# A two-layer graph attention kernel: folding W1 with the attention vectors on TensorE before the edge counts, and two reorderings on VectorE

## Chip, cores and metric

The kernel runs on one NeuronCore of a Trainium2 chip. The metric is the device time of one launch in microseconds (us). Each program was run several times; the median of the runs is what is compared. One more execution was taken by the hardware profiler.

## What is computed

There are 1250 nodes with 768 features, 20000 edges sorted by destination, and one self loop per node. The reference, cut to what matters:

```python
def _gat_layer(x, src, dst, W, a_src, a_dst, bias, concat):
    h = (x @ W).reshape(N, H, C)
    al_s = jnp.einsum('nhc,hc->nh', h, a_src)
    al_d = jnp.einsum('nhc,hc->nh', h, a_dst)
    e = leaky_relu(al_s[src] + al_d[dst], 0.2)
    m = segment_max(e, dst);  ex = exp(e - m[dst])
    alpha = ex / (segment_sum(ex, dst)[dst] + 1e-16)
    out = segment_sum(h[src] * alpha[:, :, None], dst)
    return (out.reshape(N, H * C) if concat else out.mean(axis=1)) + bias
h   = elu(_gat_layer(x, src, dst, W1, as1, ad1, b1, concat=True))    # 4 heads of 512
out = _gat_layer(h, src, dst, W2, as2, ad2, b2, concat=False)        # 1 head of 768
return layernorm(x + out)
```

## The kernel before, in words

Nodes are cut into 10 blocks of 125. The edges become a dense matrix of counts `C[source, block, destination]` (16 bit, in SBUF), and attention is then dense: for every head and every pair of source block and half of the destinations ("chunk", 625 columns) the kernel makes exp(leaky_relu(score) - shift) times the count, and TensorE multiplies it with the features. An fp32 product is made of three fp32r matmuls of high and low parts (`products`, lines 1597 to 1599), so every operand is split: ScalarE copies the high part, VectorE (or GpSimd, for W1) subtracts it to get the low part. Each engine's program is a hand-written list, run in order; engines meet only at semaphores. The stages:

- **Start.** SyncE loads the edges and then x. VectorE and ScalarE make `oh_lo`, the one-hot rows of all edges (16 and 4 groups of 8 slots: lines 1238, 948 and 951). VectorE works out a plan, which slots belong to which window.
- **Counts.** 30 windows of about 42 destination columns (`for w in range(NW)`). Per window: ScalarE shifts a table (`shift_table`), VectorE compares it with the edge keys (`one_hots`, line 1286, 7 ops), TensorE multiplies (`window`, line 1628, 7 matmuls) into one of three PSUM banks, ScalarE copies the counts out (`strip_out`). Every fourth window the engines load plan values into registers. Among the windows: the blocks of x are transposed on TensorE and split (`transpose_x`, `split_xT`, blocks at windows 1 to 10), SyncE stores the split x to DRAM (`xT_scratch`, line 624) for later heads, ScalarE splits head 0's W1, and for every block of counts TensorE transposes a strip (`transpose_counts`), and ScalarE turns it into a mask of -1e30 or 0 (`mask_out`, lines 966 to 976) and stores it on its own queue. The mask has one SBUF buffer `nbs`.
- **h of head 0.** `h_block(j)` makes 125 rows of x @ W1 with 18 matmuls, in two PSUM banks in turn; `split_h` on ScalarE and VectorE makes its high and low part. Among the first 8 blocks VectorE runs `fold(n)`: 48 reductions of 128x512 that give `wa_f` = W1 times the attention vectors (line 1272). For them SyncE loads W1 a second time in 12 pieces.
- **Scores and maxima of head 0.** `score_rows` (54 matmuls, x times `wa`), transposes of the result (`al`), `spread` over the partitions (line 1658), a copy to `srow`, and then 10 `maxima` on VectorE (line 1317), with h blocks 8 and 9 beside them. `dve_shift` makes the shift, TensorE spreads it (`gbc_ps`), ScalarE copies it to `grow`, and chunk 0 goes through GpSimd (`pool_add`), ScalarE (`act_exp`), VectorE (`dve_counts`), ScalarE (`act_hi`) and VectorE (`dve_lo`) before TensorE can use it.
- **Chunks.** 80 chunks: 4 heads, 2 halves g of the destinations, 10 source blocks b. In the half g = 1, TensorE also makes block b of the next head's h after chunk b (`make`, line 1736). Block 9 goes to the PSUM bank of block 7, so `make(h, 9)` waits with `pe.wait_ge(h_lo, NB * h + b - 1)` until VectorE has split block 7. After each half VectorE normalises the five PSUM accumulators (`evict_group`, lines 1366 to 1373). The order on VectorE is

```python
                dve_lo(dve, c)
                dve_counts(dve, c + 1)
                if b == 0 and c >= NB:
                    evict_group(c // NB - 1)
                if g == 0 and b < 3 and h > 0:
                    split_h(NB * h + NB - 3 + b)      # blocks 7, 8, 9
```

- **Layer 2.** h @ W2, scores, then 20 chunks (`CHUNKS` to `CHUNKS + 19`) in two halves. TensorE starts the second half when VectorE has evicted the first two accumulators of the first half (`evict2(0)`, `evict2(1)`, line 1539; `pe.wait_ge(y_b, 2)`). Then layer norm and stores.

Of the kernel before, what the change touches and what calls it, by code (L numbers as in the profile page):

```python
# [26 lines left out]
B = 125  # L27
# [24 lines left out]
FH = 2  # L52
# [14 lines left out]
XW = 2  # L67
# [43 lines left out]
def gat_kernel(nc, x, src, dst, W1, as1, ad1, b1, W2, as2, ad2, b2, out):  # L111
# [8 lines left out]
    with ExitStack() as ctx:  # L120
# [63 lines left out]
        wa_f = sb("wa_f", [128, KD, 2 * H], F32)  # L184
        wahi = sb("wahi", [128, KD, 2 * H], F32R)
        walo = sb("walo", [128, KD, 2 * H], F32R)
        assert cursor[0] <= base1 + XA0
# [5 lines left out]
        cursor[0] = base_attr + 2 * H * HC * 4 + 3 * 32 * KD * 2 + 2 * HC * 2  # L193
        table = sb("table", [B, TR, WM], U16)
        tab0 = sb("tab0", [B, NB, WD[0]], U16)
        strip_at = cursor[0]
        strip = sb("strip", [B, NB, B], BF16)
        nbs = sb("nbs", [B, N], BF16)
# [6 lines left out]
        cursor[0] = base_attr  # L205
        attr = sb("attr", [128, 2 * H, HC], F32)
        junk_w = sb("junk_w", [128, 2, HC], BF16)
        assert cursor[0] <= strip_at
# [16 lines left out]
        nbm = sb("nbm", [B, MR, N], BF16)  # L225
        drow = sb("drow", [B, N], F32)
# [8 lines left out]
        ehi = sb("ehi", [B, SLOTS], F32)  # L235
# [13 lines left out]
        assert cursor[0] <= prologue_end  # L249
# [62 lines left out]
        ld_att = sem("ld_att")  # L312
        ld_wk = [sem(f"ld_wk{i}") for i in range(3)]
# [5 lines left out]
        nb_stored = sem("nb_stored")  # L319
# [43 lines left out]
        wa_done = sem("wa_done")  # L363
# [9 lines left out]
        bc_ps = sem("bc_ps")  # L373
        bc_sb = sem("bc_sb")
# [230 lines left out]
        def _(sp):  # L605
            sp.dma_start(dst_i[:], dst.rearrange("(p u e) -> p u e", u=2, e=B)).then_inc(ld_dst, 16)
            sp.dma_start(src_i[:], src.rearrange("(p u e) -> p u e", u=2, e=B)).then_inc(ld_src, 16)

            for i in range(NB // XL):
                for lo, hi in ((0, XP), (XP, B)):  # L610
                    sp.dma_start(xall[lo:hi, XL * i:XL * (i + 1), :], x[XL * i * B:XL * (i + 1) * B, :]
                                 .rearrange("(b p) d -> p b d", p=B)[lo:hi, :, :]).then_inc(ld_x[i], 16)
# [12 lines left out]
            sp.wait_ge(ranges, 1)  # L625
            sp.dma_start(attr[:, 0:H, :], as1.rearrange("(o h) c -> o h c", o=1).broadcast_to([128, H, HC])
                         ).then_inc(ld_att, 16)
            sp.dma_start(attr[:, H:2 * H, :], ad1.rearrange("(o h) c -> o h c", o=1).broadcast_to([128, H, HC])
                         ).then_inc(ld_att, 16)
# [14 lines left out]

            def load_nb(h, b):
                i = NB * h + b
                if i >= MR:
                    sp.wait_ge(mx_done, i - MR + 1)
                for lo, hi in RP:
# [25 lines left out]
            def load_srow(h):  # L675
                sp.wait_ge(mx_done, NB * h)
# [169 lines left out]
        def _(pool):  # L846
# [13 lines left out]
            pool.iota(tab0[:], [[N, NB], [1, WD[0]]], base=0, channel_multiplier=0).then_inc(consts, 1)  # L860

# [67 lines left out]
        def _(act):  # L929
# [921 lines left out]
```

## Time and profile before

| | |
|---|---|
| median of 3 runs | 1021.4 us (1019.59 to 1021.71) |
| profiled execution, its own time | 1014.29 us |
| its span, first to last instruction | 1012.4 us |
| mean granted TensorE clock | 0.95 |
| TensorE matmul busy | 878.1 us, 87% |
| VectorE busy | 632.8 us, 63% |
| ScalarE busy | 420.3 us, 42% |
| GpSimd busy | 248.5 us, 25% |

Times in a trace are us from the start of the span. The clock is a share of 2.4 GHz: 1.00 is the full clock and 0.50 is 1.2 GHz. PE is TensorE's matmuls, PEld its weight loads, DVE VectorE, ACT ScalarE, POOL GpSimd, SP SyncE, and a name with a q is the queue of that engine that issues its DMAs. TensorE is busy most of the time from 240 us on; the first 240 us are the part in which it is not.

### The profile page before, as it was taken

The page shows a single profiled execution, that of the slowest core. Times are in us where ns is not written, and L with a number is a line of the kernel's source. Part 1 is how long each engine was busy: PE and PEld are TensorE (multiplying, and loading weights), DVE is VectorE, ACT ScalarE, POOL GpSimd, SP SyncE. Part 2 cuts the span into 40 slices and gives each one's busy share as a digit, 9 for nine tenths or more (in the row PEclk, how much of TensorE's full clock was granted, in tenths as well). Part 3 has the DMA queues.
Part 4 walks back from the last instruction along what each step waited for, and adds up shares of the span by engine and source line. Part 5 has one row for each costly group of instructions (what it writes and reads, how often), then busy time and mean ns, then how long its engine had stood idle before and what let it go on. Part 6 is the DMA issues. An engine that isn't in the chain of part 4 may idle for free.

```text
span 1012.4 us, 14907 instructions
## 1 busy us (share of the span) xinstructions
PE 878.1 (87%) x5572; PEld 801.9 (79%) x5572; DVE 632.8 (63%) x1229; ACT 420.3 (42%) x680; POOL 248.5 (25%) x165
## 2 busy tenths in 40 slices
PE   0675678857999899998999989899999999799797
PEld 0454456546998799887988879899999999799797
DVE  9576539464787368954789439766222344497884
ACT  6253332115653276533765338655111111287300
POOL 1002000004821245212552218540000000154451
PEclk9996879987999999998999999999999999889899
DMA  6019985456254613655226512358314332300222
GB/s 158 1 53 187 167 206 178 133 139 169 75 155 146 212 61 97 201 167 144 72 62 210 139 43 92 115 153 202 81 46 84 64 56 54 75 20 1 77 90 63
DMA packets 62983, 112.62 MB, mean 111 GB/s; under 512 B 31743, under 2 KB 33403, under 8 KB 61282
## 3 DMA queue, kind: packets, MB, share of 16 engines
q1 hardware_dynamic: 61373, 108.55, 41.5%
q10 hardware_dynamic: 1540, 3.13, 1.2%
q8 instruction: 45, 0.74, 0.4%
q14 instruction: 25, 0.20, 0.1%
HBM read 86.71 MB, written 24.94 MB: 110 GB/s over the span
## 4 chain that ended last, share of the span: by engine, by line
PE 57%; DVE 17%; issue 10%; ACT 6%; POOL 6%; DMA 3%; DVEq 1%; ACTq 0%; POOLq 0%; SPq 0%
PE ps L1597 17%; PE ps L1599 17%; PE ps L1598 17%; POOL pbuf L564 4%; DVE pbuf L577 4%; DMA mask_scratch<-nbs 3%; DVE junk_w L1272 2%; DVE vbuf L1356 2%; PE ps L1628 2%; PE ps L1708 2%; DVE PTlo L591 2%; DVE vbuf L1349 1%; DVE vbuf L1350 1%; DVE junk L1317 1%; POOL W1lo L865 1%
## 5 line engine op out<-in xcount | busy, mean ns | idle before, releaser
L564 POOL TENSOR_TENSOR pbuf<-pbuf,grow 125x625 f32<-125x625 f32 x100 | 164.9, 1650 | 632.7 <-ACT pbuf L549 242.8
L1597 PE MATMUL ps<-hx,PThi 125*125 125x260 f32 (+5 forms) x800 | 228.9, 286 | 13.2 <-DVE PTlo L591 9.3
L1599 PE MATMUL ps<-hx,PTlo 125*125 125x260 f32 (+5 forms) x800 | 226.6, 283 | 0.0
L1598 PE MATMUL ps<-hlo,PThi 125*125 125x260 f32 (+4 forms) x800 | 226.1, 283 | 0.0
L1597 PEld LDWEIGHTS ps<-hx,PThi 125*125 125x125 f32 x800 | 150.1, 188 | 17.8 <-issue 11.1
L1598 PEld LDWEIGHTS ps<-hlo,PThi 125*125 125x125 f32 x800 | 150.5, 188 | 1.4
L1599 PEld LDWEIGHTS ps<-hx,PTlo 125*125 125x125 f32 x800 | 150.2, 188 | 0.0
L577 DVE SCALAR_TENSOR_TENSOR pbuf<-pbuf,counts 125x625 f32<-125x625 f32 x100 | 111.0, 1110 | 31.6 <-ACT pbuf L571 31.4
L591 DVE TENSOR_TENSOR PTlo<-pbuf,PThi 125x625 fp32r<-125x625 f32 x80 | 77.7, 971 | 57.7 <-ACT PThi L586 57.5
L586 ACT ACTIVATE PThi<-pbuf 125x625 fp32r<-125x625 f32 x80 | 58.0, 725 | 133.9 <-PE ps L1599 67.2
L1597 PE MATMUL ps<-W2p,hT 128*125 128x384 f32 x320 | 109.7, 343 | 3.2 <-DVE hT L1362 1.7
L1599 PE MATMUL ps<-W2p,hT 128*125 128x384 f32 x320 | 108.1, 338 | 0.0
L1598 PE MATMUL ps<-W2p,hT 128*125 128x384 f32 x320 | 108.0, 338 | 0.0
L571 ACT ACTIVATE pbuf<-pbuf,s_sl 125x625 f32<-125x625 f32 x100 | 81.1, 811 | 38.2 <-POOL pbuf L564 38.1
L1362 DVE TENSOR_TENSOR hT<-ps,hT 128x500 fp32r<-128x500 f32 x40 | 25.2, 673 | 109.3 <-ACT hT L1047 109.3
L1597 PE MATMUL ps<-h2x,PT 125*125 125x384 f32 (+9 forms) x250 | 78.4, 314 | 11.0 <-DVE h2f L1508 6.8
L1597 PE MATMUL ps<-W1hi,xr 128*125 128x512 f32 x180 | 73.8, 410 | 11.6 <-DVE hlo L1253 11.6
L549 ACT ACTIVATE pbuf<-drow,s_up 125x625 f32<-125x625 f32 x100 | 80.2, 804 | 0.0
L1286 DVE TENSOR_SCALAR ring<-table,ekey 125x420 bf16<-125x420 uint16 (+1 forms) x210 | 57.0, 345 | 36.0 <-issue 18.9
L1598 PE MATMUL ps<-h2lo,PT 125*125 125x384 f32 (+7 forms) x250 | 78.0, 312 | 0.0
L1599 PE MATMUL ps<-h2x,PT 125*125 125x384 f32 (+9 forms) x250 | 78.0, 312 | 0.0
L1047 ACT ACTIVATE hT<-ps 128x500 fp32r<-128x500 f32 x40 | 21.2, 586 | 133.8 <-PE ps L1708 133.8
(175 smaller groups left out, 1636.1 us busy)
## 6 DMA issues: line engine op xcount, KB each, us to landing
xr<-xT_scratch SPq DMA_DIRECT2D x30, 750.0 KB, 4.8
nbm<-mask_scratch SPq DMA_DIRECT2D x40, 273.4 KB
hidden_scratch<-vbuf SPq DMA_DIRECT2D x40, 224.0 KB
hblk<-hidden_scratch SPq DMA_DIRECT2D x10, 896.0 KB
xT_scratch<-xa SPq DMA_DIRECT2D x20, 375.0 KB, 13.8
w1raw<-in_L_gnn_W SPq DMA_DIRECT2D x4, 1536.0 KB, 6.7
w1raw<-in_L_gnn_W SPq DMA_DIRECT2D x12, 512.0 KB, 4.4
w2raw<-in_L_gnn_W SPq DMA_DIRECT2D x14, 384.0 KB, 6.0
```

The source lines that it names most:

```text
L549: act.activation(pslot(c), src[:, g * GN:(g + 1) * GN], ACT.Relu, scale=UP, bias=bias).then_inc(z_done, 1)
L564: pool.tensor_tensor(pslot(c), pslot(c), src[:, g * GN:(g + 1) * GN], ALU.add).then_inc(e_done, 1)
L571: act.activation(pslot(c), pslot(c), ACT.Exp, scale=SLOPE, bias=bias).then_inc(p_done, 1)
L577: dve.scalar_tensor_tensor(pslot(c), pslot(c), 1.0, C[:, b, g * GN:(g + 1) * GN], ALU.min, ALU.mult).then_inc(pc_done, 1)
L586: act.activation(hi_slot(c), pslot(c), ACT.Copy).then_inc(pt_hi, 1)
L591: dve.tensor_tensor(lo_slot(c), pslot(c), hi_slot(c).bitcast(F32), ALU.subtract).then_inc(pt_lo, 1)
L1047: hi = act.activation(ht_part(n % 2, 0, a), PS[:, bank, 0:4 * B], ACT.Copy)
L1286: oh = dve.tensor_scalar(ring[:, w % 2, v, 0:win_cols(w)], table[:, w % TR, 0:win_cols(w)], ekey[:, bass.ds(at_slot(first, i, v), 1)], Non ...
L1362: lo = dve.tensor_tensor(ht_part(n % 2, 1, a), PS[:, bank, 0:4 * B], ht_part(n % 2, 0, a).bitcast(F32), ALU.subtract)
L1597: pe.matmul(dst, ahi, bhi, start=start, stop=False, skip_group_check=shared)
L1598: pe.matmul(dst[:, 0:n], ahi, blo, start=False, stop=False, skip_group_check=shared)
L1599: return pe.matmul(dst, alo, bhi, start=False, stop=stop, skip_group_check=shared)
```

## The change

1. **The fold moves to TensorE and to the start.** SyncE loads the attention vectors (32 rows of 128) and all of W1 (12 DMAs of 512 KB, in two halves) ahead of x. `fold_step(i)` transposes six 128x128 tiles of W1 into PSUM, ScalarE copies them out (`weights_out`, 128x768), and two plain fp32 matmuls with 384 columns add `acz` (the attention vectors as columns) times them. 16 units in all: steps 0 to 9 ahead of window 0 (`FS = 10`), steps 10 to 16 after windows 0 to 6. ScalarE's `weights_out` copies stand between its one-hot groups. VectorE's 48 reductions are gone, and so are the second loads of W1 and the vectors.
2. **x and head 0's W1 come later.** The blocks of x are transposed after windows 10 to 19 (`XW` 2 to 11). `load_w1(0)`, which stood ahead of the 20 stores of xT in SyncE's queue, stands behind them. ScalarE waits for it at window 22 (`WROW + 1`) and splits W1 in windows 22 to 24.
3. **Score rows among the counts.** `score_rows(0..2)` after windows 21 to 23, `al` at window 24. The `spread` of head 0's source scores is gone: `srow` is loaded from DRAM.
4. **Head 0's maxima beside h.** VectorE runs them between the splits of blocks 0 to 8; h block 9 comes after the `spread` of the shift. `b1row`, for which VectorE waits ahead of its first `dve_lo`, is still loaded once all ten blocks are made.
5. **Two mask buffers** `nbs` instead of one, with a semaphore each.
6. **`split_h` ahead of `evict_group`** on VectorE.
7. **`evict2(0)`, `evict2(1)`** two chunks earlier in the second layer.

The diff, cut to its core:

```diff
-XW = 2
+XW = 11
+FS = 10
+FU = 16
...
+            sp.dma_start(an[0:FU, :], as1.rearrange("h (t p) -> (h t) p", p=128)).then_inc(ld_an, 16)
+            sp.dma_start(an[FU:2 * FU, :], ad1.rearrange("h (t p) -> (h t) p", p=128)).then_inc(ld_an, 16)
+            for i in range(2):
+                for k in range(KD):
+                    sp.dma_start(w1f[:, 2 * i:2 * i + 2, k, :], W1[k * 128:(k + 1) * 128, 2 * i * HC:(2 * i + 2) * HC]
+                                 .rearrange("p (h c) -> p h c", h=2)).then_inc(ld_wf[i], 16)
...
-            sp.wait_ge(xt_ps, NB)
-            load_w1(0)
...
                 sp.wait_ge(xt_lo, j + 1)
                 for u in range(2):
                     sp.dma_start(xT_d[j, :, u, :].rearrange("p (k n) -> p k n", k=KD), xa[:, u, :, j, :].bitcast(F32)).then_inc(xT_stored, 16)
...
-            sp.wait_ge(xT_stored, 32 * NB)
-            sp.wait_ge(w1_hi, KD)
-            sp.wait_ge(w1_lo, KD)
-            for n in range(2 * KD):
-                if n >= 3:
-                    sp.wait_ge(wa_done, H * (n - 2))
-                sp.dma_start(w1raw[:, 2 * (n % 3):2 * (n % 3) + 2, :],
-                             W1[128 * (n // 2):128 * (n // 2) + 128, bass.ts(n % 2, 2 * HC)]
-                             .rearrange("p (a c) -> p a c", a=2)).then_inc(ld_wk[n % 3], 16)
-            sp.wait_ge(wa_done, 2 * H * KD)
-            load_w1(1)
+            load_w1(0)
...
-            sp.wait_ge(nb_stored, RS * NB)
-            for b in range(MR):
-                load_nb(0, b)
             sp.wait_ge(rows_sb, 3)
             sp.dma_start(rows_d[:, :], rows[:]).then_inc(rows_stored, 16)
             sp.wait_ge(rows_stored, 16)
+            load_srow(0)
+            for b in range(MR - 1):
+                load_nb(0, b)
+            sp.wait_ge(strip_done, NW)
             load_drow(0, 0)
+            sp.wait_ge(ct_ps, NB)
+            load_drow(0, 1)
+            load_nb(0, MR - 1)
             for b in range(MR, NB):
                 load_nb(0, b)
-            sp.wait_ge(rows_ps, 3)
+            sp.wait_ge(w1_lo, KD)
+            sp.wait_ge(xT_stored, 32 * NB)
+            load_w1(1)
             sp.wait_ge(mk_done, NB)
-            load_drow(0, 1)
             for lo, hi in RP:
                 sp.dma_start(b1row[lo:hi, :], spread_row(b1, hi - lo)).then_inc(ld_b1, 16)
...
-                if b >= 1:
-                    act.wait_ge(nb_stored, RS * b)
-                act.activation(nbs[:, 0:2 * CW].rearrange("p (a n) -> p a n", a=2), PS[0:B, 3:5, 0:CW], ACT.Copy,
+                if b >= 2:
+                    act.wait_ge(nb_stored[b % 2], RS * (b // 2))
...
+            def weights_out(u):
+
+                act.wait_ge(wt_ps, u + 1)
+                act.activation(wT[:, u % 2, :].rearrange("p (a k) -> p a k", a=2), PS[:, 3:5, 0:DH], ACT.Copy).then_inc(wt_sb, 1)
+
...
+            attention_columns()
+            weights_out(0)
+            weights_out(1)
             act.wait_ge(ekeys, 2)
             for g in range(LA):
                 slot_ones(g)
+                weights_out(2 + 2 * g)
+                weights_out(3 + 2 * g)
             for w in range(NW):
                 if w + TR - 1 < NW:
                     shift_table(w + TR - 1)
                 if XW <= w < XW + NB:
                     split_xT(w - XW)
                 strip_out(w)
+                if FS + w < FU:
+                    weights_out(FS + w)
...
+                if WROW < w <= WROW + 3:
+                    score_rows_out(w - WROW - 1)
+                    if w == WROW + 1:
+                        act.wait_ge(ld_w1, 16)
+                    split_w1(2 * (w - WROW) - 2)
+                    split_w1(2 * (w - WROW) - 1)
...
+            strip_of(NB - 1)
+            for j in range(NB - 1):
+                split_h(j)
+                if j in (1, 2):
+                    maxima(0, j - 1)
+                if 3 <= j < 7:
+                    maxima(0, 2 * j - 4)
+                    maxima(0, 2 * j - 3)
+                if j == 7:
+                    dve.wait_ge(al_sb, 1)
+                    dve_shift(dve, 0, al[:, H, :])
+            split_h(NB - 1)
             dve_counts(dve, 0)
...
                     dve_counts(dve, c + 1)
+                if g == 0 and b < 3 and h > 0:
+                    split_h(NB * h + NB - 3 + b)
                 if b == 0 and c >= NB:
                     evict_group(c // NB - 1)
-                if g == 0 and b < 3 and h > 0:
-                    split_h(NB * h + NB - 3 + b)
...
-                if c == CHUNKS + 2 * NB - 1:
+                if c == CHUNKS + 2 * NB - 3:
                     evict2(0)
                     evict2(1)
...
+            def fold_step(i):
+
+                if i < FU:
+                    if i % (FU // 2) == 0:
+                        pe.wait_ge(ld_wf[i // (FU // 2)], 16 * KD)
+                    if i >= 1:
+                        pe.wait_ge(wt_sb, i)
+                    for k in range(KD):
+                        t = pe.transpose(PS[:, 3 + k // 3, k % 3 * 128:(k % 3 + 1) * 128],
+                                         w1f[:, i // 4, k, i % 4 * 128:(i % 4 + 1) * 128], ident[:, :])
+                    t.then_inc(wt_ps, 1)
+                if i >= 1:
+                    u = i - 1
+                    if u == 0:
+                        pe.wait_ge(acz_done, 1)
+                        pe.wait_ge(ekeys, 2)
+                    pe.wait_ge(wt_sb, u + 1)
+                    for a in range(2):
+                        t = pe.matmul(PS[0:2 * H, 5 + 2 * a, 0:DH], acz[:, u, :], wT[:, u % 2, a * DH:(a + 1) * DH],
+                                      start=u == 0, stop=u == FU - 1)
+                    if u == FU - 1:
+                        t.then_inc(wrow_ps, 1)
             pe.wait_ge(plan, 6)
             pe.transpose(PS[0:2 * NW, 6, 0:PAIRS], key[:].rearrange("p v w -> p (v w)"), ident[0:PAIRS, 0:PAIRS]
                          ).then_inc(keys_ps, 1)
             pe.wait_ge(keys_red, 1)
-            pe.transpose(PS[0:1, 5, 0:2 * NW], kred[:], ident[0:2 * NW, 0:2 * NW]).then_inc(keys_row, 1)
+            pe.transpose(PS[0:1, 6, 2 * PAIRS:2 * PAIRS + 2 * NW], kred[:], ident[0:2 * NW, 0:2 * NW]).then_inc(keys_row, 1)
+            for i in range(FS):
+                fold_step(i)
...
-                    pe.wait_ge(strip_done, NW)
+                    pe.wait_ge(al_sb, 1)
...
+                if FS + w <= FU:
+                    fold_step(FS + w)
                 if XW - 1 <= w < XW - 1 + NB:
+                    if w == XW - 1:
+                        pe.wait_ge(wa_lo, 1)
                     transpose_x(w - XW + 1)
-            for j in range(HB):
+                if WROW <= w < WROW + 3:
+                    score_rows(w - WROW)
+                if w == WROW + 3:
+                    pe.wait_ge(rows_sb, 3)
+                    for j in range(NB):
+                        t = pe.transpose(PS[0:B, 7, 2 * H * j:2 * H * (j + 1)], rows[:, j * B:(j + 1) * B],
+                                         ident[0:2 * H, 0:2 * H])
+                    t.then_inc(al_ps, 1)
...
+            for j in range(NB - 1):
                 h_block(j)
                 if j < 2:
                     transpose_counts(NB - 2 + j)
-            pe.wait_ge(wa_hi, 1)
-            pe.wait_ge(wa_lo, 1)
             pe.wait_ge(nbs_done, NB)
-            for c in range(3):
-                score_rows(c)
-            pe.wait_ge(rows_sb, 3)
-            for j in range(NB):
-                t = pe.transpose(PS[0:B, 5, 2 * H * j:2 * H * (j + 1)], rows[:, j * B:(j + 1) * B],
-                                 ident[0:2 * H, 0:2 * H])
-            t.then_inc(al_ps, 1)
-            pe.wait_ge(al_sb, 1)
-            spread(lambda b: al[:, 0, b:b + 1], four_from(2)).then_inc(bc_ps, 1)
-            for j in range(HB, NB):
-                h_block(j)
-            pe.wait_ge(bc_sb, 1)
+            pe.wait_ge(strip_done, NW)
             pe.wait_ge(g_done, 1)
             spread(lambda b: gcol[:, b:b + 1], four_from(2)).then_inc(gbc_ps, 1)
+            h_block(NB - 1)
```

## Rows read from the trace of the kernel before

**Rows 1.** Busy time per engine in stretches of the prologue (start and end us).

```profile
core 0: us, PE busy (x) PEld busy (x) DVE busy (x) ACT busy (x) POOL busy (x), PEclk, DMA share, GB/s
30.10:71.10 41.00, 32.26 (x183) 23.18 (x183) 30.12 (x104) 19.81 (x43) 0.00 (x0) 0.96 0.03 9
71.10:148.10 77.00, 49.27 (x229) 33.03 (x228) 40.09 (x135) 28.78 (x58) 7.47 (x6) 0.73 1.10 195
148.10:192.00 43.90, 36.45 (x164) 27.44 (x164) 34.19 (x105) 7.42 (x13) 0.00 (x0) 1.00 0.51 161
192.00:238.80 46.80, 27.01 (x141) 18.99 (x141) 19.61 (x40) 10.23 (x18) 3.03 (x3) 0.85 0.58 154
```

**Rows 2.** Timeline of the start: begin, duration, engine, line, [idle before <- what ended it].

```profile
10.09 16.73 DVE L1238 TENSOR_TENSOR oh_lo<-colid,elo 125x1000 bf16<-125x1000 uint16 x15
10.60 2.41 ACT L948 ACTIVATE oh_lo<-colid,elo 125x125 bf16<-125x125 uint16 x8
...
14.08 2.41 ACT L948 ACTIVATE oh_lo<-colid,elo 125x125 bf16<-125x125 uint16 x8
...
30.13 0.58 PE L1620 MATMUL ps<-zcols,ident_b 125*125 125x420 bf16 x1 [22.46 <-issue]
```

**Rows 3.** Tile h2f, its copy out of PSUM: ns min/median/max.

```profile
L1084 ACT ACTIVATE h2f<-ps x10: 810/822/822, 706.3 to 871.0; 125x768 f32<-125x768 f32 x10
```

**Rows 4.** Timeline of TensorE: transposes and a window.

```profile
63.58 0.84 PE L1588 MATMUL ps<-ident,xall 125*128 125x125 f32 x6
...
102.68 1.42 PE L1628 MATMUL ps<-ring,oh_lo 125*125 125x420 bf16 x7
```

**Rows 5.** Groups by line up to 260 us: the spread of `al` (busy us, mean ns).

```profile
L1658 PE MATMUL ps<-ident,al 125*125 125x125 f32 x20 | 2.4, 277 | 0.3 <-ACT al L1015 0.3
```

**Rows 6.** ScalarE's timeline: one wait for a mask store.

```profile
112.83 1.00 ACT L971 ACTIVATE nbs<-ps 125x1000 bf16<-125x1000 f32 x1 [5.14 <-DMA mask_scratch<-nbs]
```

**Rows 7.** Tile xT_scratch (issue ns min/median/max), and engines and DMA in two stretches.

```profile
L624 SPq DMA_DIRECT2D xT_scratch<-xa x20: 545/2588/4356, 71.1 to 120.6; - x20
```

```profile
82.00:132.00 50.00, 34.25 (x158) 22.77 (x157) 28.96 (x95) 20.31 (x40) 7.47 (x6) 0.74 1.22 158
137.00:142.00 5.00, 1.04 (x3) 0.61 (x4) 1.60 (x7) 2.98 (x6) 0.00 (x0) 0.74 0.99 379
```

**Rows 8.** TensorE alone in the score rows (clock, DMA, GB/s), then timeline to chunk 0.

```profile
192.80:203.00 10.20, 10.20 (x54) 1.00 0.24 69
```

```profile
209.10 0.06 DVE L1316 MEMSET gate<- 125x1 f32 x1 [16.40 <-ACT srow L982]
...
226.87 4.53 PE L1658 MATMUL ps<-ident,gcol 125*125 125x125 f32 x20 [10.84 <-DVE gcol L601]
238.77 0.55 PE L1597 MATMUL ps<-hx,PThi 125*125 125x260 f32 x1 [7.37 <-DVE PTlo L591]
```

**Rows 9.** Change of head 0 to 1, then 1 to 2: timeline, and TensorE's clock.

```profile
339.07 0.60 ACT L942 ACTIVATE hx<-ps 125x512 fp32r<-125x512 f32 x1 [2.01 <-PE ps L1599]
...
348.60 0.16 DVE L1338 TENSOR_SCALAR deps<-ps 125x2 f32<-125x2 f32 x1 [11.40 <-PE ps L1599]
...
354.06 0.51 PE L1597 MATMUL ps<-W1hi,xr 128*125 128x512 f32 x1 [3.73 <-DVE hlo L1253]
...
474.82 0.79 PE L1597 MATMUL ps<-W1hi,xr 128*125 128x512 f32 x1 [3.94 <-DVE hlo L1253]
```

```profile
474.80:480.70 5.90, 5.88 (x14) 0.50 0.00 0
```

**Rows 10.** Second layer, between its halves, and the wait near the end: timeline.

```profile
941.03 0.81 DVE L577 SCALAR_TENSOR_TENSOR pbuf<-pbuf,counts 125x625 f32<-125x625 f32 x1 [0.22 <-ACT pbuf L571]
...
947.86 0.15 DVE L1496 TENSOR_SCALAR deps<-ps 125x1 f32<-125x1 f32 x1
...
951.13 0.68 PE L1597 MATMUL ps<-h2x,PT 125*125 125x384 f32 x1 [6.78 <-DVE h2f L1508]
...
995.49 0.16 DVE L1496 TENSOR_SCALAR deps<-ps 125x1 f32<-125x1 f32 x1 [4.81 <-PE ps L1599]
```

More of the change, by code:

```diff
@@ L66 @@
 XP = 112
-XW = 2
+XW = 11
+FS = 10
+FU = 16
+WROW = 21
 XR = 3
@@ L311, in gat_kernel @@
         ld_w1 = sem("ld_w1")
-        ld_att = sem("ld_att")
-        ld_wk = [sem(f"ld_wk{i}") for i in range(3)]
+        ld_an = sem("ld_an")
+        ld_wf = [sem(f"ld_wf{i}") for i in range(2)]
         xT_stored = sem("xT_stored")
@@ L318, in gat_kernel @@
         rows_stored = sem("rows_stored")
-        nb_stored = sem("nb_stored")
+        nb_stored = [sem(f"nb_stored{i}") for i in range(2)]
         g_stored = sem("g_stored")
@@ L860, in _ @@
             pool.iota(tab0[:], [[N, NB], [1, WD[0]]], base=0, channel_multiplier=0).then_inc(consts, 1)
+            pool.memset(acz[:], 0.0).then_inc(consts, 1)
             def split_w1(h, k):
@@ new lines, in attention_columns @@
+            def attention_columns():
+                act.wait_ge(ecol_ps, 1)
+                act.wait_ge(consts, 9)
+                for h in range(H):
+                    for v in range(2):
+                        lo = (v * H + h) * 4
+                        last = act.activation(acz[:, 4 * h:4 * h + 4, v * H + h], PS[:, 0, lo:lo + 4], ACT.Copy)
+                last.then_inc(acz_done, 1)
+            def weights_out(u):
+                act.wait_ge(wt_ps, u + 1)
+                act.activation(wT[:, u % 2, :].rearrange("p (a k) -> p a k", a=2), PS[:, 3:5, 0:DH], ACT.Copy).then_inc(wt_sb, 1)
@@ new lines, in folded_rows_out, with score_rows_out @@
+            def folded_rows_out():
+                act.wait_ge(wrow_ps, 1)
+                act.activation(warow[:, 0:DH], PS[0:2 * H, 5, 0:DH], ACT.Copy)
+                act.activation(warow[:, DH:D], PS[0:2 * H, 7, 0:DH], ACT.Copy).then_inc(wrow_sb, 1)
+            def score_rows_out(c):
+                act.wait_ge(rows_ps, c + 1)
+                act.activation(rows[:, TCH[c][0] * B:TCH[c][1] * B],
+                               PS[0:2 * H, 6 + c % 2, 0:(TCH[c][1] - TCH[c][0]) * B], ACT.Copy).then_inc(rows_sb, 1)
@@ L1260, in strip_of @@
                 dve.tensor_scalar(strip[:], C[:, :, b * B:(b + 1) * B], 1.0, None, ALU.min).then_inc(strip16, 1)
-            def fold(n):
-                k, half = n // 2, n % 2
-                if n == 0:
-                    dve.wait_ge(ld_att, 32)
-                    dve.wait_ge(win_done, NW)
-                dve.wait_ge(ld_wk[n % 3], 16 * (n // 3 + 1))
-                for i, v in enumerate((2 * half, H + 2 * half, 2 * half + 1, H + 2 * half + 1)):
-                    if 4 * n + i >= 2:
-                        dve.wait_ge(wa_done, 4 * n + i - 1)
-                    dve.tensor_tensor_reduce(out=junk_w[:, i % 2, :], in0=w1raw[:, 2 * (n % 3) + i // 2, :],
-                                             in1=attr[:, v, :], scale=1.0, scalar=0.0, op0=ALU.mult, op1=ALU.add,
-                                             accum_out=wa_f[:, k, v:v + 1]).then_inc(wa_done, 1)
             def one_hots(w, first, count, before):
@@ L1299, in _ @@
                     strip_of((w - 5) // 3)
-            for j in range(HB):
-                if j == 0:
-                    strip_of(NB - 1)
-                for n in range(FH * j, min(FH * j + FH, 2 * KD)):
-                    fold(n)
-                split_h(j)
-            dve.wait_ge(wa_hi, 1)
-            dve.tensor_tensor(walo[:], wa_f[:], wahi[:].bitcast(F32), ALU.subtract).then_inc(wa_lo, 1)
+                if w == FU - FS + 3:
+                    dve.wait_ge(wa_hi, 1)
+                    dve.tensor_tensor(walo[:], PS[:, 7, 0:2 * H * KD].rearrange("p (k v) -> p k v", k=KD), wahi[:].bitcast(F32), ALU.subtract
+                                      ).then_inc(wa_lo, 1)
             def maxima(h, b):
@@ L1311, in maxima @@
                 dve.wait_ge(ld_nb[i % MR], RS * (i // MR + 1))
-                if b == 0 and h > 0:
-                    dve.wait_ge(ld_srow, RS * h)
+                if b == 0:
+                    dve.wait_ge(ld_srow, RS * (h + 1))
                 if i >= 1:
@@ L1318, in maxima @@
                                          op0=ALU.add, op1=ALU.max, accum_out=mx[:, i:i + 1]).then_inc(mx_done, 1)
-            dve.wait_ge(al_sb, 1)
-            dve.wait_ge(bc_sb, 1)
-            for b in range(NB):
-                if b in (3, 5):
-                    split_h(HB + (b - 3) // 2)
-                maxima(0, b)
-            dve_shift(dve, 0, al[:, H, :])
+            strip_of(NB - 1)
[9 more added lines that the diff above has]
+                    dve_shift(dve, 0, al[:, H, :])
+            split_h(NB - 1)
             dve_counts(dve, 0)
```

114 lines of the change are left out of this document (60 added, 54 removed).

## The prediction

> **What bounds the kernel now.** I read the engine table first: TensorE is the engine with the most to do, so the question is where it waits. The stretches of the prologue [rows 1] show it: from 240 us on TensorE is nearly full, but the 46.8 us before chunk 0 hold 27.0 us of matmuls, the 43.9 us of head 0's h hold 36.5, and the 77.0 us of the last 18 windows hold 49.3 at a granted clock of 0.73. Then I read the chain of waits, line by line, at three places: the prologue, the change of head, and the second layer between its halves. The prologue is one chain: one-hots, 30 windows, 8 h blocks at VectorE's fold pace (43.9 / 8 = 5.5 us a block), score rows, spread, maxima, shift, first chunk. Whatever moves chunk 0, which starts at 238.8, moves the end by as much, since TensorE is full behind it.
>
> **The start gets longer.** Window 0 begins at 30.1: VectorE's one-hots end at 26.8 and the plan values take 3.3 more [rows 2]. Now TensorE must also do fold steps 0 to 9, which need the first half of W1 (3.1 MB), and ScalarE does ten copies in between. In 137 to 142 us, when pieces of W1 were loaded, DMA moved 379 GB/s; in 82 to 132, with the small rows of xT, 158 [rows 7]. That bounds the first half at 8 and 20 us; with issue and landing it is there at 12 to 24, and I take 13, by the row of the same kind of load. A copy is a 128x768 one out of PSUM, 0.82 us [rows 3]. Transposes of a unit take 0.84 us at full clock (twice that at half) [rows 4]; a plain fp32 pass of 125 columns takes 2.4 / 20 = 0.12 us [rows 5], two passes a matmul, so by columns 384 of them twice for two matmuls is 1.5 us at most; if the pass is bound by its weight load instead, half of that. I take 1.3. ScalarE's groups of one-hots repeat every 3.48 us [rows 2]. It does nothing of them before copies 0 and 1, which end some 5 us after W1 has landed. Then four times a group, a copy, TensorE's transposes, a copy: 3.48 + 0.82 + 0.95 + 0.82 = 6.1, with handshakes 6.3; then copies 8 and 9, the last matmul and the plan load. 13 + 5 + 25 + 1 + 3.3: window 0 begins at about 47, **17 us later**. x lands behind all of W1, 6.3 MB: at 31 to 60 by the same two rates, ahead of its first use below.
>
> **The counts.** Of the windows' cost this much is taken: 12 windows with 10 blocks of x took 41.0 us, 3.4 each; the other 18 took 77.0, 4.3 each [rows 1]. In the second group the mask buffer costs, 5.14 us in one such wait [rows 6] of which there are three, and the idle TensorE is at half clock. Two buffers remove those waits. A window's 7 matmuls take 1.42 us at full clock [rows 4], about 1.5 with its first and last. A window with a fold step is 1.5 + 0.84 + 1.3 = 3.7 on TensorE, and seven have one; windows 7 to 10 take some 2.4; two plan loads, the wait for the folded rows and half clock at the first ones add 12. So the first x block is transposed at 47 + 26 + 10 + 12 = 95 and split at about 100. From there SyncE's queue counts: 20 stores of xT at 2.59 us of issue each [rows 7], 52 us in which the DMA engines are full (share 1.22 [rows 7]), and `load_w1(0)` now stands behind them. Its 1.6 MB at 379 GB/s take 4.2, landing and ramp 2.5: W1 is there at 100 + 52 + 7 = **158.5**. By TensorE's work (11 windows at 3.4 from 100, and 4 us of score rows at each of two) ScalarE would reach window 22 at about 145, so it stops there, and with it the copies of counts, hence windows 25 on, the score rows' copies and `al`. After the landing ScalarE needs 6 us for windows 22 to 24 with six W1 splits, and five windows at 3.4 are 17: h begins at 181.5, against 148.1.
>
> **h, maxima and chunk 0.** 22,500 columns of score rows took 10.2 us [rows 8], 0.453 ns each, so an h block (18 x 512) is 4.2 us. Nine blocks and the last two count transposes are 39 us: TensorE's pace, since VectorE's two maxima per block (10 took the 17 us from 209.1 to the spread at 226.9 [rows 8]: 3.4 us a pair and 0.7 for the split) just fit in 4.2. The 16.4 us that VectorE waited at 192.7, the score rows among them, and the 17 us of maxima are gone from the path. After the spread (2.4 at full clock against 4.53) stand 7.4 us to chunk 0 as before [rows 8], and 1.2 more because VectorE splits block 9 ahead of the counts of chunk 0. But `b1row` (1 MB) is asked for only when block 9 is made, 6.6 us after the spread begins; 0.7 to issue, 2 to land, 2.7 at 379 GB/s, and `dve_lo` behind it give 13 us from spread to chunk 0. Chunk 0 starts at 181.5 + 39 + 13 = 233.7: the whole prologue gives **5 us**, 33 lost ahead of h and 38 won behind it. Behind the wait for W1 SyncE stores the score rows and loads `srow` and two masks; it can from 5 us after the landing, and the first maxima stand after h block 1, 25 us later. Masks 2 to 9 wait until mask 9 is stored, after block 1, and are wanted from block 3 on, 8 us later, against 2 to 3 us for a store or a load of 0.3 MB at 158 GB/s. `load_w1(1)` behind them is wanted at chunk 3 only. GpSimd's one memset costs nothing; it is idle there.
>
> **Change of head.** Block 7's high half is ready at 339.1 [rows 9], but VectorE waits 11.4 us in front of `evict_group` until 348.6, normalises and only then splits block 7; TensorE, done with its chunk, waits 3.73 us for it, until 354.06. There are three such places: 3.73, 3.94 and one more like the second. Behind the gap the clock is at half: 5.9 us of it at the second, which costs 3 us [rows 9], half of that at the other two: 6 in all. With the split first, it is done at 340.3 (339.1 and twice 0.6), `make(h, 9)` runs during the normalising, and the normalised accumulators are ready when it ends: next late is nothing, for the following chunk's `dve_lo` was done before and ScalarE's next step is released by TensorE itself. 11.6 + 6 = 17.6; I take **17**, 9 to 18.
>
> **Second layer.** VectorE runs the two evictions from 947.86 and TensorE starts its second half 6.78 us late, then at half clock [rows 10]. Two chunks earlier VectorE is free at 941.84; TensorE ended the first half at 951.13 - 6.78 = 944.3, and its last step finishes the accumulators one by one over some 5 us, the two first ones by 942; 3.1 us of evictions end at 945.0, 6.1 us earlier, and about 2 us of half clock are saved. The three delayed `dve_lo` are needed later than they come. At the end VectorE, with 4.81 us to spare [rows 10], becomes the later one. I take **6.5**, 4 to 8.
>
> Sum: 5 + 17 + 6.5 = 28.5. It is made against the profiled execution, 1014.3 (span 1012.4), which lies 7.1 under the median of the runs, 1021.4. Taken off that median: **993**.
>
> **Rivals.**
> - *The queue does not bind (0.17).* If xT drains faster without the vector loads and with fewer masks between, or windows keep a full clock, the counts run at TensorE's pace and h begins at 171: 10.5 us less, 982. For it: TensorE's load in the counts is the smaller sum. Against: 2.59 us an issue.
> - *Fold partly at half clock (0.18).* ScalarE and TensorE hand over to each other, TensorE idle in between. Half of the next rival's cost, 16 us: 1009.
> - *Slower: fold and first windows at 1.2 GHz throughout (0.07).* Start 5 us later, seven windows at 7.4 for 3.7 add 26, four at 1.5 more 6, less 4 already counted: x's first split at 133, W1 at 191, chunk 0 at 267; 28 lost against 23.5 won, 1026. It decides when x's first block is split later than 128.6. For it: clock 0.73 in the second stretch [rows 1]; against: 0.96 in the first, where transposes of x stand in every window.
> - *The change of head does not pay (0.12).* Another wait takes its place, as ScalarE's or VectorE's chain for chunks 23 on. The 17 shrink to 4: 1006.
> - Something none of these names takes all of the gain: 0.03.
>
> The Trainium skill ("TensorE: Matmul & The Clock Gate", Part 4) says that transposes do not count as activity for the clock gate, which speaks against this change: by that rule the fold steps, a third or more transposes, would be at 1.2 GHz, the slower rival's 1026. This case's 0.96 with six transposes in ten of the first twelve windows speaks against it.
>
> **The numbers.** The forecast has 0.43. About 0.2% (2 us) is what a measurement of this kernel can tell from no change. Faster 0.90 (all but the slower rival and the last), same 0.02, slower 0.08. The range takes in the first rival and the two at 1006 and 1009: 979 to 1010; the forecast's own is 985 to 1001.
>
> **What would show it.** Window 0 at 47; x's first split at 100; `w1raw` landing at 158 with ScalarE idle before W1's first high copy; h block 0 at 181; chunk 0 at 234 with VectorE waiting for `b1row`; no wait of TensorE for `hlo` at the three changes of head, and full clock there; TensorE's gap before the second half under 1.5 us. Wrong if W1's first half lands after 20, if the clock in the fold is 0.5, or if a new wait stands before chunks 20, 40, 60.

## The result, and the profile after

The changed kernel takes **991.1 us** (median of 4 runs, 988.64 to 991.75), the kernel before 1020.5 beside it (4 runs, 1019.59 to 1021.71): a ratio of 0.9707, 95% interval 0.9689 to 0.9724. Forecast were 993 us and a range of 979 to 1010. The profiled execution took 991.75 us, its span is 989.8 and its mean granted clock 0.96.

First the prologue again in stretches, whose borders are the same events as in [rows 1]: window 0, first store of xT, W1(0) in SBUF, first h block, chunk 0.

```profile
core 0: us, PE busy (x) PEld busy (x) DVE busy (x) ACT busy (x) POOL busy (x), PEclk, DMA share, GB/s
0.00:44.90 44.90, 25.97 (x103) 11.77 (x103) 24.81 (x48) 24.75 (x58) 3.00 (x14) 1.00 0.78 230
44.90:90.40 45.50, 38.55 (x204) 23.53 (x204) 23.33 (x90) 20.65 (x39) 0.00 (x0) 0.92 0.05 15
90.40:159.50 69.10, 49.68 (x265) 33.57 (x265) 32.85 (x114) 23.10 (x48) 0.00 (x0) 0.82 1.08 153
159.50:183.40 23.90, 15.81 (x74) 11.69 (x75) 14.47 (x37) 11.97 (x26) 7.49 (x6) 0.66 0.25 68
183.40:236.40 53.00, 45.49 (x224) 36.66 (x221) 23.89 (x47) 14.75 (x24) 4.31 (x3) 0.98 0.48 140
```

What was weak is the same in kind and sits elsewhere. The 69.1 us of xT's stores have full DMA engines (share 1.08) at 153 GB/s, with TensorE busy for 49.7 of them. The 53 us from the first h block to chunk 0 hold 45.5 us of matmuls; in [rows 1] the last two stretches, 90.7 us, held 63.5.

The timeline of the same execution, TensorE, ScalarE and VectorE in order of time:

```profile
14.42 1.54 PE L1604 MATMUL ps<-ident,w1f 128*128 128x128 f32 x6 [6.61 <-DMA w1f<-in_L_gnn_W]
16.00 0.81 ACT L997 ACTIVATE wT<-ps 128x768 f32<-128x768 f32 x1 [9.96 <-PE ps L1604]
18.33 2.73 PE L1614 MATMUL ps<-wT,acz 128*8 128x384 f32 x4
...
22.35 1.46 PE L1614 MATMUL ps<-wT,acz 128*8 128x384 f32 x4
23.74 0.88 PE L1604 MATMUL ps<-ident,w1f 128*128 128x128 f32 x6
...
44.93 0.36 PE L1665 MATMUL ps<-zcols,ident_b 125*125 125x420 bf16 x1 [1.10 <-issue]
...
159.64 1.15 ACT L944 ACTIVATE W1hi<-w1raw 128x512 fp32r<-128x512 f32 x2 [10.17 <-DMA w1raw<-in_L_gnn_W]
164.28 2.26 PE L1740 MATMUL ps<-ident,rows 8*125 8x8 f32 x10 [7.42 <-ACT rows L1008]
...
222.37 2.34 PE L1707 MATMUL ps<-ident,gcol 125*125 125x125 f32 x20
235.33 0.81 DVE L600 TENSOR_TENSOR PTlo<-pbuf,PThi 125x625 fp32r<-125x625 f32 x1 [4.37 <-DMA b1row<-in_L_gnn_b]
236.40 0.55 PE L1642 MATMUL ps<-hx,PThi 125*125 125x260 f32 x1 [7.51 <-DVE PTlo L600]
...
337.89 0.69 DVE L1286 TENSOR_TENSOR hlo<-ps,hx 125x512 fp32r<-125x512 f32 x1 [1.95 <-ACT hx L948]
346.80 0.16 DVE L1357 TENSOR_SCALAR deps<-ps 125x2 f32<-125x2 f32 x1 [8.21 <-PE ps L1644]
348.36 0.40 PE L1642 MATMUL ps<-W1hi,xr 128*125 128x512 f32 x1
...
927.80 0.44 PE L1642 MATMUL ps<-h2x,PT 125*125 125x384 f32 x1 [1.10 <-DVE h2f L1527]
```

The chain `hlo`, `evict_group`, `make(h, 9)` of [rows 9] has turned round: block 7 is split at 337.9, 8.9 us ahead of the normalising, and TensorE goes from the last matmul of its chunk into W1 at 348.36 without a gap. The 6.78 us ahead of the second layer's second half [rows 10] are 1.10. Two new waits are to be seen in the prologue, `w1raw` at 159.64 and `b1row` at 235.33.

The chain of waits, followed through the counts, says what stands behind the first of them:

```profile
136.88 0.39 DVE xa L1281
137.28 0.41 SPq L637
137.74 4.68 SPq L637
142.46 17.16 DMA w1raw<-in_L_gnn_W
159.64 1.15 ACT W1hi L944 x2
```

The last block of x is split at 137.3, the last two stores of it take 5.1 us to issue, and from the issue of W1 to its landing 17.2 us go by. The stores themselves, issued from 90.4 on, and among them the last two (the landing times are those of the two issued at 137.3 and 137.7):

```profile
L637 SPq DMA_DIRECT2D xT_scratch<-xa x20: 359/546/4682, 90.4 to 137.7; - x20
DMA to landing us min/median/max: 14.7/16.0/17.4
```

The first store landed 4.9 us after its issue, the last 17.4, at 155.1, and W1 4.5 us behind it. In all six profiles with W1 behind the 20 stores it landed 3.8 to 4.8 us after the last of them.

Stage by stage, from four profiles, two of each kernel (the second of each is among the experiments):

| stage | before | after | gain |
|---|---|---|---|
| start of the span to chunk 0 | 238.8, 240.1 | 236.4, 237.5 | 2.5 |
| to VectorE's normalising of head 2 | 352.6, 353.7 | 342.9, 341.3 | 11.1 |
| to the second half of layer 2 | 359.7, 360.9 | 348.5, 348.4 | 11.9 |
| to the end | 61.3, 61.6 | 62.0, 62.0 | -0.6 |

They add up to 24.9 us. The medians differ by 29.4. The first profile of before, 1014.3, is 5.3 us under the lowest of the four timed runs of before. On which chip it was taken is not on record; on the chip of the first experiments the kernel before took 1014.3 to 1018.0, so there it would be nothing unusual.

### The profile page after: what moved, and what is told of

Read it like the earlier page. It is cut to its first block, busy times and chain, and to the rows that moved or that the text cites. A ratio compares the mean times of both kernels' runs of the same rounds, so it can differ in the third digit from the quotient of the medians.

```text
span 989.8 us, 15130 instructions
## 1 busy us (share of the span) xinstructions
PE 898.7 (91%) x5719; PEld 809.6 (82%) x5719; DVE 606.7 (61%) x1133; ACT 431.9 (44%) x704; POOL 249.9 (25%) x166
## 4 chain that ended last, share of the span: by engine, by line
PE 60%; DVE 17%; issue 7%; ACT 7%; POOL 4%; DMA 3%; SPq 1%; DVEq 1%; ACTq 0%; POOLq 0%
PE ps L1642 17%; PE ps L1644 17%; PE ps L1643 17%; DVE pbuf L586 4%; POOL pbuf L573 3%; PE ps L1673 3%; DVE vbuf L1375 2%; DVE PTlo L600 2%; DMA w1raw<-in_L_gnn_W 2%; PE ps L1762 2%; PE ps L1614 2%; DVE vbuf L1368 1%; PE ps L1604 1%; DVE h2f L1553 1%; DVE vbuf L1369 1%
## 5 line engine op out<-in xcount | busy, mean ns | idle before, releaser
L1644 PE MATMUL ps<-hx,PTlo 125*125 125x260 f32 (+5 forms) x800 | 227.4, 284 | 0.0
L586 DVE SCALAR_TENSOR_TENSOR pbuf<-pbuf,counts 125x625 f32<-125x625 f32 x100 | 114.0, 1140 | 26.3 <-ACT pbuf L580 26.2
L871 POOL TENSOR_TENSOR W1lo<-w1raw,W1hi 128x512 fp32r<-128x512 f32 x24 | 39.8, 1669 | 156.6 <-ACT W1hi L944 156.6
```

Source lines behind the costliest of these rows:

```text
L586: dve.scalar_tensor_tensor(pslot(c), pslot(c), 1.0, C[:, b, g * GN:(g + 1) * GN], ALU.min, ALU.mult).then_inc(pc_done, 1)
L871: pool.tensor_tensor(W1lo[:, bass.ds(k, 1), :], w1raw[:, bass.ds(k, 1), :], W1hi[:, bass.ds(k, 1), :].bitcast(F32), ALU.subtract).then_inc ...
L1644: return pe.matmul(dst, alo, bhi, start=False, stop=stop, skip_group_check=shared)
```

## The experiments

Each was timed in five or more runs beside the kernel before on the same chip. Ratios are compared, since the kernel before took 1016.4 us on the chip of the first four experiments, 1022.1 on that of the next four and 1020.2 on that of the last three.

**The kernel before against itself.** What can be told from nothing?

> The kernel before, unchanged, for a second profile and for the noise of the comparison. The changed kernel's median is 29.4 us below the median of before, but the two profiled executions differ by 22.5 (1014.3 to 991.8). Theory A, the first profile of before was an execution on the fast side of its scatter: this profile lies at 1018 to 1022 with the extra time spread over the clock's ups and downs, and the ratio is 1.000 within 0.2%. Theory B, the medians are off and the profile is typical: this profile lies at 1014 again.

1018.3 us, ratio 1.0016 (1.0003 to 1.0028). The bound of 0.2% holds for the ratio, just, and not for the whole interval. The profile is one of 1018.2 us, as theory A had it, and its extra 3.9 us are spread: 1.3 ahead of chunk 0, 1.1 and 1.2 in the next two stages, 0.3 at the end.

**Block 7's split alone.** The kernel before with

```diff
+                if g == 0 and b < 3 and h > 0:
+                    split_h(NB * h + NB - 3 + b)
                 if b == 0 and c >= NB:
                     evict_group(c // NB - 1)
-                if g == 0 and b < 3 and h > 0:
-                    split_h(NB * h + NB - 3 + b)
```

> Before, with only the split of blocks 7 to 9 set ahead of evict_group. My sum gave this 17 us (three gaps, 11.6, and the half clock behind them, 6). From the two profiles the three changes of head gave 15.3. Theory A: 15 to 18 us faster (ratio 0.983 to 0.985), TensorE has no wait for hlo in the changes of head. Rival, the gain belongs to the new prologue as well (the later chunks only keep up because the early stages ended sooner): less than 10.

1000.5 us, ratio 0.9841 (0.9826 to 0.9856): 16.2 us. In its timeline the split stands ahead of the normalising, none of the three changes of head has a wait of TensorE, and the second layer's gap is still there:

```profile
339.72 0.69 DVE L1253 TENSOR_TENSOR hlo<-ps,hx 125x512 fp32r<-125x512 f32 x1 [2.19 <-ACT hx L942]
...
348.62 0.16 DVE L1338 TENSOR_SCALAR deps<-ps 125x2 f32<-125x2 f32 x1 [8.21 <-PE ps L1599]
...
934.27 0.69 PE L1597 MATMUL ps<-h2x,PT 125*125 125x384 f32 x1 [6.72 <-DVE h2f L1508]
```

**`evict2` alone.** The kernel before with

```diff
-                if c == CHUNKS + 2 * NB - 1:
+                if c == CHUNKS + 2 * NB - 3:
                     evict2(0)
```

> Before, with only evict2(0) and evict2(1) two chunks earlier. My sum gave 6.5 us; the two profiles show the start of TensorE's second half 5.6 us nearer and 0.7 of it lost by the end. Theory A: 4.5 to 6.5 us faster (ratio 0.9936 to 0.9956), TensorE's gap about 1 us. Rival, VectorE sets the end of the kernel: under 2 us.

1012.3 us, ratio 0.9954 (0.9941 to 0.9968): 4.7 us. The wait ahead of the second half fell to 1.77 us.

**The prologue alone.** The changed kernel with both edits above taken back.

> The changed kernel with both reorderings of VectorE undone: only the new prologue. My sum gave it 5 us; the two profiles show chunk 0 starting 2.4 us earlier. Theory A, the parts add up and the profile is typical: 2 to 3 us faster (ratio 0.997 to 0.998). Theory B, the prologue is worth what the medians leave over (29.4 less 15.3 less 5): 7 to 9 us faster (0.991 to 0.993).

1009.0 us, ratio 0.9920 (0.9905 to 0.9935): 8.1 us, 6.6 to 9.7. In its profile h begins at 180.1 and chunk 0 at 232.8; the waits at the changes of head are back (3.74, 3.72, 3.71 us). The three ratios multiplied give 0.9717, the whole change 0.9707: within the intervals the parts add, and none hides another. Of the two theories the second, 7 to 9 us, came true.

**W1 ahead of the last stores.** The changed kernel with

```diff
             for j in range(NB):
-                sp.wait_ge(xt_lo, j + 1)
+                sp.wait_ge(xt_lo, j + 1 if j < 6 else NB)
+                if j == 6:
+                    load_w1(0)
                 for u in range(2):
...
-            load_w1(0)
```

> The changed kernel, with head 0's W1 asked for after 6 of the 10 blocks of xT are stored (once all x is transposed) and not behind all 20 stores. In the changed kernel ScalarE waited 10.2 us for it at window 22 and TensorE 7.4. Theory A, the queue of xT stores set the time of h: W1 lands near 141 and not 159.6, ScalarE does not wait, h begins 8 to 11 us earlier, ratio to before 0.960 to 0.963. Rival, the counts had other work to wait for (VectorE's plan loads, ScalarE's longer list): h begins less than 4 us earlier, ratio 0.967 or more.

980.0 us against 1022.1, ratio 0.9593 (0.9575 to 0.9612), 0.0114 or 11.7 us below the changed kernel. h begins at 174.5, chunk 0 at 227.4. SyncE's timeline, and under it the landing of `w1raw`'s four loads from its tile's view, here and in the changed kernel:

```profile
138.15 0.37 SPq L631 DMA_DIRECT2D w1raw<-in_L_gnn_W  x1
138.57 21.33 SPq L639 DMA_DIRECT2D xT_scratch<-xa  x8
```

```profile
DMA to landing us min/median/max: 6.8/8.1/9.5
```

```profile
DMA to landing us min/median/max: 6.8/8.1/17.2
```

W1 is issued only 4.3 us sooner than in the changed kernel (142.46), since the edit makes it wait for x's last block. But the eight last stores are not ahead of it: it lands in 9.5 us in place of 17.2, and ScalarE, which has the score rows' and counts' copies to do first, doesn't wait for it at all: it splits W1 from 150.2 on in place of 159.6. The sooner issue alone could have given 4.3 of these 9.4 us. SyncE issues no store from 120.7 to 138.2 here, and the twelve stores before had landed by 131.3, so W1 meets no backlog. So it was mostly the stores already handed to the DMA engines that set h. With that wait gone the counts' own pace sets it.

**`b1row` off the first chunk.** The changed kernel, with VectorE's wait for `b1row` (all that uses it is the normalising) moved from its first `dve_lo` to the first line of the first eviction:

```diff
-            dve.wait_ge(ld_b1, RS)
...
                 h, n = q // 2, GT * q + t
+                if n == 0:
+                    dve.wait_ge(ld_b1, RS)
```

> The changed kernel, with VectorE's wait for b1row moved from ahead of chunk 0 to the first eviction, where b1row is first read. In the changed kernel VectorE waited 4.37 us for it. Theory A: chunk 0 starts 3.5 us earlier and all of it is kept, ratio 0.967. Rival, the first chunks are paced by GpSimd and ScalarE and the gain is gone by chunk 10: under 1 us.

991.2 us, ratio 0.9703 (0.9681 to 0.9726): no difference from the changed kernel that this can tell. Its VectorE doesn't wait:

```profile
232.91 0.81 DVE L600 TENSOR_TENSOR PTlo<-pbuf,PThi 125x625 fp32r<-125x625 f32 x1 [0.79 <-ACT PThi L595]
```

and from the first h block to chunk 0 there are 49.4 us in place of 53.0. The 3.6 us are real in the profile; in it h begins 1.2 us later.

**One mask store at a time.** The changed kernel, in which each mask waits for the store of the one ahead of it, as the single buffer did.

```diff
-                if b >= 2:
-                    act.wait_ge(nb_stored[b % 2], RS * (b // 2))
+                if b >= 1:
+                    act.wait_ge(nb_stored[(b - 1) % 2], RS * ((b + 1) // 2))
```

> The changed kernel, in which every mask waits for the store of the one ahead of it, as with one buffer. Theory A, the two buffers paid because stores of masks take 10 us behind the stores of xT while three windows take less: windows 13 to 20 get 3 to 6 us longer, but W1 lands when it did, since the queue sets that, so the end moves by less than 2 us. Rival, the mask waits are on the path: 4 us or more slower than the changed kernel (ratio 0.975).

993.4 us, ratio 0.9723 (0.9701 to 0.9745): 1.6 us above the changed kernel, within the two intervals. Its waits between 40 and 150 us (in total, times, longest) have one line for it:

```profile
ACT nbs L977 <- DMA mask_scratch<-nbs: 0.9, 1, 0.9
```

The 5.14 us of [rows 6] don't come back when the second buffer's use is taken away. Theory A is half right: the end hardly moves, but not because the queue hides longer windows.

**One-hots ahead of the first copies.** The changed kernel, ScalarE making two groups of one-hots before copies 0 and 1 of W1, when it only waits for W1 (9.96 us at 16.00), and three copies after each later group.

```diff
-            weights_out(0)
-            weights_out(1)
             act.wait_ge(ekeys, 2)
-            for g in range(LA):
+            slot_ones(0)
+            slot_ones(1)
+            for u in range(4):
+                weights_out(u)
+            for g in range(2, LA):
                 slot_ones(g)
-                weights_out(2 + 2 * g)
-                weights_out(3 + 2 * g)
+                for u in range(3):
+                    weights_out(3 * g - 2 + u)
```

> The changed kernel, with ScalarE's first two groups of one-hots ahead of its first copies of transposed W1. In the changed kernel ScalarE sat idle 10.0 us ahead of copy 0 (until 16.0) and window 0 began at 44.9. Theory A: window 0 begins 5 to 7 us earlier, the first block of x and so the queue of xT stores and W1 as well, and h with them: ratio 0.964 to 0.966. Rival, TensorE's own ten fold steps (24 us from 14.4) set window 0: 3 us or less.

993.3 us, ratio 0.9715 (0.9692 to 0.9738): nothing gained. Window 0 is 1.9 us earlier (42.99), xT's first store is where it was, and the 20 stores took longer, although the last block of x was split at 135.8, 1.5 us sooner than in the changed kernel:

```profile
90.59 57.51 SPq L637 DMA_DIRECT2D xT_scratch<-xa  x20
```

**The changed kernel once more, and two sums of the above,** on one chip: W1 ahead with `b1row` late, and both with the one-hots first.

> The changed kernel unchanged, once more, as the yardstick for its variants in the same call. My theory (a real gain of about 29 us with some scatter in the drain of the xT stores): ratio 0.969 to 0.973, the issue of the 20 xT stores 49 to 58 us long in its profile, h's first block 144 us or so after window 0 less or more by what that drain takes (180 to 187). Rival (the first result was lucky or unlucky in its chip): a ratio outside 0.968 to 0.974.

> load_w1(0) after six of the ten blocks of xT stores, as in the run of W1 ahead (0.9593), and VectorE's wait for b1row moved to the first eviction. If only the drain of the xT stores hid what b1row cost in the timed runs, the 3.6 us that its profile kept from h on now reach the end: 0.9593 less 0.0035, ratio 0.954 to 0.957, chunk 0 some 49.5 us after h's first block instead of 53. Rival (something behind chunk 0 absorbs it, so that the wait for b1row cost nothing): 0.958 to 0.961 with the same 49.5 us.

> As the one before, and two groups of ScalarE's one-hots ahead of its first two copies of W1. The earlier run of that alone had window 0 2 us sooner and gave nothing, because the xT stores took longer. If the queue was what hid it, those 2 us now reach h: window 0 at 43 to 43.5, h's first block at 172 to 173, ratio 0.951 to 0.955. Rival (the counts' own work between window 0 and h depends on when the stores run, so an earlier start is given back there): window 0 at 43, h still at 174 to 176, ratio as the one before.

| | us | ratio | window 0 | first xT store | h | chunk 0 |
|---|---|---|---|---|---|---|
| changed kernel | 991.4 | 0.9710 (0.9683 to 0.9738) | 45.2 | 91.8 | 184.5 | 237.5 |
| W1 ahead, `b1row` late | 976.6 | 0.9571 (0.9551 to 0.9591) | 44.7 | 89.9 | 172.8 | 222.1 |
| and one-hots first | 975.5 | 0.9559 (0.9541 to 0.9578) | 42.8 | 89.8 | 173.6 | 223.0 |

The result repeats. Between h and chunk 0 both sums have the 49.4 us without `b1row`. Against W1 ahead alone (0.9593) the first is 2.2 us faster, less than the 3.6 of the profiles, and the intervals overlap; its ratio lies on the border between the two expectations, so how much of `b1row` reaches the end isn't settled. The one-hots gain nothing that can be told (1.1 us), and here the profile says where they go: the time from window 0 to the first store of xT, in windows of the two sums

```profile
44.70:89.90 45.20, 38.24 (x204) 23.21 (x204) 23.24 (x90) 20.66 (x39) 0.00 (x0) 0.92 0.05 15
```

```profile
42.80:89.80 47.00, 40.00 (x204) 24.18 (x204) 23.37 (x90) 20.65 (x39) 0.00 (x0) 0.89 0.05 14
```

is 1.8 us longer in the second, with the same 204 matmuls at a lower clock. That was the rival's place. But this stretch takes 45.2 to 47.0 in the seven profiles that have no such edit, so that the edit causes it is not shown. Of the 1.8 us 1.6 lie in window 0 (7.1 us to window 1 against 5.5), behind which the second sum has a stretch at half clock from 45.5 to 48.9 and the first none; of the seven profiles five have such a stretch.

## Why the prediction was right, point by point

**The start: right, 2 us long.** W1's half was there at 14.4 (13 forecast), copies 0 and 1 ended at 19.3 (18), the cycle of one-hots and two copies took 6.2 us (19.14 to 25.36 on ScalarE; 6.3), and window 0 came at 44.9, not 47: ahead of it TensorE shows 1.10 us of issue where I had taken 3.3 for the plan values. Transposes of a unit at 0.88 and its two matmuls at 1.46 us, in four passes, are the 0.84 and "1.5 at most" of the text; I took 1.3. x was not late: from 27 to 35 us the DMA share is 1.04, from 35 to 45 it is 0.22, long before x is wanted at 85.7. The upper bound that I gave for it, 60, was too low by its own rate: 10.1 MB at 158 GB/s take 64 us of transfer alone.

**The counts: three terms wrong, and they cancelled.** Windows 1 to 6 follow one another at 3.66 us, as summed (3.7). But the 12 us for plan loads, the folded rows and half clock were about 5: the first block of x is transposed at 85.7, not 95, and stored from 90.4, not 100. Then I had W1 behind 52 us of issue and 7 of landing. The stores' issue did end 52.0 us after it began, but by luck. I had taken 2.59 us for each; half of them now took 0.55 or less, and all 20 together 17.7. SyncE issued in bursts and waited for x's splits in between, the last of which came at 137.3. That was the counts' pace, which I also had too fast: windows 12 to 19 took 5.0 us each in place of 3.4, at a granted clock of 0.76 (90.4 to 137.3). What I had too small is the landing, 17.2 us in place of 7, because the 20 stores, 7.5 MB of short rows, were still landing until 155.1, 64.7 us after the first was issued, and W1 came 4.5 us behind them. Ten us early and ten us late gave 159.6 for 158.5: luck. The statement "the queue sets h" was right in its effect, as W1 ahead showed with 11.7 us, and wrong in its mechanism: not the time of issuing counts, but what the DMA engines still hold. The rival in which it doesn't bind (982) is refuted for this kernel. Its price, 10.5 us, is near what lifting it was worth: with W1 ahead h begins at 174.5, against the 171 of the rival.

The Trainium skill ("DMA: Bandwidth & Descriptors", Specifications) wants transfers of at least 512 bytes for the full rate. The rows of xT are 125 fp32 values, 500 bytes, and the trace fits: 153 GB/s at a DMA share of 1.08, against 388 GB/s at 1.05 for W1's long rows (14.4 to 20.9 us). It doesn't prove the rule: the first are stores and the second loads, and no run varied the row length alone.

**h to chunk 0: right.** From the landing to h 23.8 us (23 forecast), h block to h block 4.2, h to spread 38.9 (39), spread to chunk 0 14.0 (13), of which 4.37 are VectorE's wait for `b1row`. VectorE's maxima fit beside h.

**The prologue as a whole: 5 forecast, 8.1 timed** (6.6 to 9.7), 2.5 in the pair of profiles and 7.2 in the profile of the prologue alone against that of the kernel before again (240.1 and 232.8). The same instructions begin h at 180.1 in one profile and at 183.4 and 184.5 in two others, with W1 landing in 16.4, 17.2 and 18.3 us: the term is no constant but has the scatter of the stores' drain in it. I had given a single number. The sum, 28.5 for a measured 29.4, is nearer than its parts: 5, 17 and 6.5 were 8.1, 16.2 and 4.7, so here too errors cancelled.

**The two mask buffers: credited for nothing.** "Two buffers remove those waits" put the end of the 5.14 us waits on the second buffer; with its use taken away one wait of 0.9 us is left. In the new order the mask stores have more time between them: while xT is being stored ScalarE's mask copies begin 11.3 to 17.8 us apart (102.4 to 146.7), without a wait, against 12.0 to 12.3 before, of which 4.3 to 5.2 were the wait. It changed no number, since either cause removes them.

**Change of head: right, 17 against 16.2.** The chain was shown by the split alone, and nothing was late next, against the rival's 1006.

**Second layer: right in mechanism, 6.5 against 4.7** (timed alone; 4 was my lower bound). Before the second half 1.10 us are left of 6.78 (forecast: under 1.5), and the end gives 0.6 us back, where VectorE is now the later engine (its waits of 4.81 and 2.10 us near the end are gone). I had named that and not priced it.

**The clock.** The two rivals at half clock (1009, 1026) didn't come true. The slower one needed x's first split later than 128.6; the first store, which follows it, is at 90.4. From 23.74 on six transposes take 0.88 us, and from window 0 to the first store the granted clock is 0.92. The first units were at half rate all the same: 1.54 us for six transposes and 2.73 for four passes, in a stretch that the row gives as 1.00. The trace's records of the clock begin only at 22.2 us, and up to the first record the row shows 1.00. The 0.96 of [rows 1], on which the prediction leaned, is too high for the same reason: the records of that trace begin at 37.0, and the first window's seven matmuls took 2.71 us against the 1.42 of [rows 4], as long as seven of them took in the changed kernel at 46.58, at a recorded 0.50:

```profile
31.99 2.71 PE L1628 MATMUL ps<-ring,oh_lo 125*125 125x420 bf16 x7 [1.28 <-DVE ring L1286]
```

The Trainium skill's rule that transposes don't count for the clock gate ("TensorE: Matmul & The Clock Gate", Part 4) is not tested by this trace: fp32 matmuls of 384 columns, 1.46 us of them, stand between every six transposes and may be what held the clock. What the prediction drew from the rule, a fold at 1.2 GHz throughout, didn't come: 0.88 us for the six is the full rate.

## What to carry to other kernels

Moving work only pays as far as the next fixed event, so look for it first: here the landing of W1, for which ScalarE waited 10.2 us. For a load behind stores, sum the bytes that the DMA engines still hold when it is issued, not only the queue's issue times, and put the one load that is waited for ahead of stores that nobody waits for. A split that frees a PSUM bank goes ahead of a normalising for which nobody waits yet: two lines moved gave more than half of the gain.

## What the runs showed of the hardware

- A granted clock of 1.00 at the start of a trace can mean that there is no record yet. The first two transpose groups of the fold took 1.54 us each and the first four passes 2.73, against 0.88 (from 23.74) and 1.46 (from 22.35) later. The clock records begin at 22.2 us in this trace, and between 21.6 and 37.9 in all thirteen.
- Stores of 500-byte rows that are still landing delay a load behind them by 7 to 10 us: landing 16.0 to 19.3 us in the six profiles with W1 behind all of them, at most 9.5 in the three with it ahead of eight and the earlier twelve landed.
- The same kernel took 1016.4 us on one chip and 1022.1 on another, 0.6% apart, nearly as much as the prologue's 0.8%: only ratios from one chip could tell the parts.
